# State-space stage of a decoder: the last two operations of each batch's layernorm on GpSimd instead of VectorE

## What is computed

```python
def _layernorm(x, axis=-1, eps=1e-05):
    m = jnp.mean(x, axis=axis, keepdims=True)
    v = jnp.var(x, axis=axis, keepdims=True)
    return (x - m) / jnp.sqrt(v + eps)
```

```python
BC = x @ W_in + b_in
Bm, Cm = (BC[..., :N], BC[..., N:])
dt = jax.nn.softplus((x @ W_dt1 + b_dt1) @ W_dt2 + b_dt2)
dt = jnp.clip(dt, 1e-07, 1000000.0)
tmp = A * dt[..., None]
A_bar = jnp.exp(tmp)
B_barX = jnp.expm1(tmp) / tmp * dt[..., None] * Bm[:, :, None, :] * x[..., None]
_, h = jax.lax.associative_scan(combine, (A_bar, B_barX), axis=1)
return jnp.sum(h * Cm[:, :, None, :], axis=-1) + D * x
```

## Time and profile before

| | us |
|---|---|
| three runs, median | 2016.48 |
| lowest, highest | 2016.09, 2019.49 |
| profiled execution, its own time | 2024.31 |
| its span, first to last instruction | 2022.6 |

### The profile page before, as it was taken

One profiled execution on the slowest core, in us unless ns is written; L12 is line 12 of the kernel. 1 busy time (PEld: TensorE's weight loads), 2 busy tenths in 40 slices (PEclk: granted clock), 3 DMA queues, 4 the chain that ended last, 5 costly groups with the idle time before them and its releaser, 6 DMA issues.

```text
span 2022.6 us, 34313 instructions
## 1 busy us (share of the span) xinstructions
PE 1636.8 (81%) x12460; PEld 1173.2 (58%) x12460; DVE 1373.1 (68%) x3111; ACT 1096.4 (54%) x2271; POOL 697.5 (34%) x773
## 2 busy tenths in 40 slices
PE   6588871737999788879898889988989987888864
PEld 5344431625777655567777767765559964555532
DVE  2577752137777699567999767759964456478876
ACT  4488850205777477538788345546764441147642
POOL 1344434167888302234665512220000020001238
PEclk9699975868999999986887899999999998979985
DMA  2200000110000000010000100000000000000000
GB/s 89 101 12 11 6 33 36 41 36 18 2 1 1 1 1 2 4 37 1 1 1 1 58 1 2 2 11 1 2 1 1 1 17 1 16 1 1 2 1 21
DMA packets 10422, 29.26 MB, mean 14 GB/s; under 512 B 2113, under 2 KB 6663, under 8 KB 9361
## 3 DMA queue, kind: packets, MB, share of 16 engines
q1 hardware_dynamic: 8210, 24.98, 3.5%
q0 software_dynamic: 2048, 2.12, 0.4%
HBM read 23.92 MB, written 5.24 MB: 14 GB/s over the span
## 4 chain that ended last, share of the span: by engine, by line
PE 41%; DVE 19%; POOL 13%; issue 8%; ACT 3%; DMA 0%; POOLq 0%; DVEq 0%; ACTq 0%
PE PS L1117 5%; PE PS L1199 4%; DVE negmax L2370 4%; PE PS L1259 3%; POOL big L738 3%; PE PS L1454 3%; PE PS L1465 3%; DVE V L2864 3%; POOL big L726 2%; POOL big L734 2%; PE PS L1700 2%; PE PS L1281 2%; DVE QS L2430 1%; PE PS L1174 1%; PE PS L1616 1%
## 5 line engine op out<-in xcount | busy, mean ns | idle before, releaser
L1900 ACT ACTIVATE big<-PS 128x1024 f32<-128x1024 f32 (+1 forms) x256 | 248.2, 971 | 135.8 <-PE PS L1210 135.2
L2370 DVE TENSOR_REDUCE negmax<-PS 128x4 f32<-128x1024 f32 x192 | 234.5, 1222 | 46.2 <-PE PS L1199 44.2
L630 POOL TENSOR_TENSOR rstd<-veps,mhalf 128x2 f32<-128x2 f32 x80 | 58.1, 726 | 397.9 <-DVE veps L2248 396.7
L1199 PE MATMUL PS<-KS,QS 32*128 32x256 f32 (+1 forms) x1152 | 134.8, 320 | 48.2 <-DVE negmax L2370 41.9
L1199 PEld LDWEIGHTS PS<-KS,QS 32*128 32x128 f32 x1152 | 86.5, 188 | 124.5 <-DVE negmax L2370 88.5
L1259 PE MATMUL PS<-big,V 128*32 128x256 f32 (+1 forms) x2048 | 134.4, 381 | 0.0
L1210 PE MATMUL PS<-QS,KS 32*128 32x256 f32 (+1 forms) x1152 | 133.1, 318 | 1.4 <-ACT big L1900 1.4
L1956 ACT ACTIVATE KS<-PS,NB,W 128x256 fp32r<-128x256 f32 x160 | 81.6, 561 | 78.3 <-PE PS L1117 49.2
L656 POOL TENSOR_TENSOR res<-resb,XB 128x256 f32<-128x256 f32 x24 | 17.4, 727 | 303.9 <-ACT resb L1970 303.9
L1956 ACT ACTIVATE QS<-PS,NB,W 128x256 fp32r<-128x256 f32 x160 | 81.6, 561 | 40.7 <-PE PS L1117 40.7
L1117 PE MATMUL PS<-xT,W 128*128 128x256 f32 x320 | 90.4, 407 | 13.3 <-ACT xT L1939 11.3
(11 more groups left out here) (412 smaller groups left out, 4530.5 us busy)
## 6 DMA issues: line engine op xcount, KB each, us to landing
W<-in_wpack SPq DMA_DIRECT2D x1, 4180.0 KB, 13.6
W<-in_wpack SPq DMA_DIRECT2D x1, 2836.5 KB, 9.2
W<-in_wpack SPq DMA_DIRECT2D x1, 2560.0 KB, 8.6
W<-in_wpack SPq DMA_DIRECT2D x3, 772.0 KB, 5.2
mask_i<-in_mask SPq DMA_DIRECT2D x8, 256.0 KB, 2.7
W<-in_wpack SPq DMA_DIRECT2D x1, 1798.0 KB, 6.9
x_tok<-in_x SPq DMA_DIRECT2D x1, 1024.0 KB, 4.9
ctxT<-in_ctx SPq DMA_DIRECT2D x1, 1024.0 KB, 7.7
```

Of the source, the lines that this page charges most:

```text
L1199: mm = nc.tensor.matmul(PS[:, MAXB[half], o], QS[r, bm % 2, tm, j * P:(j + 1) * P], KS[r, bm % 2, tm, k], start=not a.causal, stop=last)
L1900: nc.scalar.activation(PX[:, T % 2, 2 * p:2 * p + 2, 0:cols], PS[:, exp_banks(g)[0]:exp_banks(g)[0] + 2, 0:cols], ACT.Exp, scale=a.scale). ...
L2370: ins = nc.vector.tensor_reduce(negmax[:, h:h + 2, :].rearrange("p h j -> p (h j)"), banks.rearrange("p h (j k) -> p (h j) k", j=2), AX.X, ...
```

## The change

`norm(b)` goes from VectorE's loop, two scalar_tensor_tensor a batch at t = 4b + 7. GpSimd does the two operations at t = 4b + 6, in `root(b)`, as tensor_scalar with two per-partition scalars, behind a wait for its own root and ahead of `gains(4b+7)`. The last of them signals `x_done`.

```diff
@@ GpSimd, L2a, root(b)
                     own.step(nc.gpsimd.tensor_scalar(veps[:, :], mv[:, :, 1], 1e-5, 1.0, ALU.add, ALU.mult))
                     nc.gpsimd.tensor_tensor(rstd[:, :], veps[:, :], mhalf[:, :], ALU.pow).then_inc(sem("rstd"), 1)
+                    pool.wait_ge(sem("rstd"), before(n, "rstd") + b + 1)
+                    for j in range(2):
+                        ins = nc.gpsimd.tensor_scalar(x_tok[:, 2 * b + j, :], res[:, j, :], mv[:, j, 0:1], rstd[:, j:j + 1],
+                                                      ALU.subtract, ALU.mult)
+                    ins.then_inc(x_done, 1)
@@ VectorE, L2a
-                def norm(b):
-                    dve.wait_ge(sem("rstd"), before(n, "rstd") + b + 1)
-                    for j in range(2):
-                        ins = nc.vector.scalar_tensor_tensor(x_tok[:, 2 * b + j, :], res[:, j, :], mv[:, j, 0:1],
-                                                             rstd[:, j:j + 1].broadcast_to([P, P]), ALU.subtract, ALU.mult)
-                    ins.then_inc(x_done, 1)
-
                 for t in range(SCAN_FIRST, SCAN_LAST):
                     if t == 4 * B:
                         scalings("L2x")
-                    if (b := due(t, SCAN_DONE, 4)) is not None:
-                        norm(b)
                     if (b := due(t, SCAN_Y, 4)) is not None:
                         residual(b)
```

## The result

The changed kernel took 2036.65 us, median of four runs (2030.53 to 2037.42), against 2017.34 (2016.09 to 2019.49) for the kernel before. The ratio on record is 1.0074, 95% interval 1.0044 to 1.0104 (it isn't the quotient of the two medians, which is 1.0096): slower by both, where I had forecast 2012.3 us and a range up to 2018.0. The changed kernel run once more gave 2033.35 (2030.03 to 2037.78) against 2019.01 for 20 runs of before, ratio 1.0079 (1.0066 to 1.0092). The profiled execution took 2030.53 us, the lowest of the four, its span 2028.7; the other three took 2036.1 to 2037.4, and no profile of such a run was kept.

The account below looks back on a forecast made before the run. VectorE was taken to set the pace of the state-space loop, TensorE close behind. Terms -5.25 + 0.24 + 0 + 0 + 0.8 = -4.2 us gave 2020.1 profiled, carried over to 2012.3 us; range 2010.4 to 2018.0.

Parts of the forecast that it names:

- I carry the difference over: Whole kernel: the three-run median lies 7.8 us below the profiled execution, so 2020.1 there becomes 2012.3.
- the sum: State-space stage: -5.25 + 0.24 + 0 + 0 + 0.8 = -4.2 us, giving 2020.1 for the profiled execution.
- D: Batch loop: GpSimd keeps the port, L2771 waits for the multiply, +1.1 in each of five batches; 2023.5 us; chance 0.16.
- Parts 1 to 3: Batches 0 to 4: 1.05 us a batch saved, 0.53 from removal on VectorE, 0.52 from the port freed sooner; -5.25.
- Part 4: Batch 5, no scan_ratio behind it: +0.24 if the scan asks first, +2.2 more if the next multiply does.
- Part 5: Batch 6: last scan starts 1.38 us later, hidden behind TensorE's sums; taken as 0, upper end 1.0.
- Part 6: Batch 7: pair ends 1.1 us later than VectorE's, but next stage's start hangs on the residual; 0.
- Part 7: Batches 0 to 4: the earlier feed waits for TensorE, 0.5 us at the tightest, 0.3 for the other four; +0.8.

Follow-up runs that it names:

- scan 27 first: The changed kernel with one wait: gains(28) on GpSimd held until the scan of step 27 is done; median 2017.09 us, ratio 1.0003 to before.

## Why the prediction was wrong

**The step that failed** is the sentence under the sum, "I carry the difference over": I took everything outside the stage as a fixed length that moves along. L3a isn't fixed. It has two lengths 13 us apart, and less than a microsecond of work ahead of it moved a kernel from one to the other. The nine timed runs of the changed kernel were all at 2030 us or more; of the 24 of the unchanged kernel beside them one was (2030.8). For the profiled execution the sum gave 2020.1 us and 2030.53 was measured, 10.4 more: 13.1 from L3a and 3.7 from the stage (0.5 gained and not 4.2), less 5.0 ahead of the stage and 1.5 in the stages behind it other than L3a. From the profiled execution to the median I took off 7.8 us; the changed kernel's median lies 6.1 above its profiled execution, and these 13.9 us stay open, since its runs at 2036 and 2037 have no profile.

**A second step failed, and L3a covers it up**: parts 4 and 5 of the sum, +0.24 and 0, measured +5.24 and +1.29. They turn the -5.63 of batches 0 to 4 into +0.90. The -0.5 us of the first pair is luck, for scan 4 was hit in the kernel before. Against the two profiles of the unchanged stage without a stretched scan (245.5 and 245.6 us) the changed stage is 2 to 3 us longer.

The shift was too large for any of my rivals: D (2023.5, slower) was the nearest in sign, and its mechanism did not happen.

By its own parts:

- *Parts 1 to 3, batches 0 to 4*: -5.25 forecast, -5.63 measured, and the mechanism as described but for L2776. The pair ended 1.38 us after the scan (I had 1.45). L2776 started 0.21 us ahead of that end and still took 0.42 us, where I had it wait and end 0.28 behind the pair; L2778 waited, with 0.67 us. The reciprocal was undisturbed. Rival D, at 0.16, was wrong at its own point of decision: L2776 started at 1050.10, ahead of the multiply's 1050.32.
- *Part 4, batch 5*: I took +0.24 and named +2.2 as the other end. The other end came, in all five profiles in which GpSimd did batch 5's pair ahead of the multiply and without the added wait: scan 27 took 4.47 or 4.48 us. My reason, that GpSimd has a memset ahead, was wrong: the multiply started 0.02 us before the scan did. Steps 27 and 28 grew by 2.4 us, as this other end has it. What I had not priced is TensorE behind it: 3.51 us without work, then half rate, 2.86 us more in step 29, and 5.24 us in all over steps 27 to 29.
- *Part 5, batch 6*: step 31 grew by 1.29 (1.38 forecast). I took 0 for its effect on the stage; I have no run that isolates it.
- *Part 6, batch 7*: right but for some tenths. The pair ran from 1144.91 to 1146.48 us and L2x was 210.2 us against 209.8.
- *Part 7, TensorE's slack*, +0.8: not visible as such. In the changed kernel's first profile all five steps were at 7.88 or 7.89, so VectorE did not wait for TensorE there; no run shows the 0.8. The one collision, at step 16 (+1.55), is the same kind of event as in before at step 4.
- *The sum for the stage*: -4.2 forecast; -0.5 and -1.0 in two profiles. Without the last three batches it is -9.0 to -9.1, of which the five steps explain 5.6 and 2.6 lie behind the last scan (8.6 us against 11.2); this went with a higher clock of TensorE, 0.83 against 0.78, and wasn't tested apart. L2x gave 1.4 of it back. The same unchanged stage was 245.5 to 248.7 us in four profiles, so a forecast for it can't be better than about 3 us.

The sentence of the Trainium skill that I weighed, from "Perfetto Trace Analysis", section "Optimizing Scalar/DVE Operations", says that offloading between VectorE and GpSimd might not help because of the shared port. On the steps that the change touches the trace agrees: +0.90 us net. But it is a balance and no rule for each place: beside the 0.52 us for VectorE's two instructions, the order on the port gave 0.61 us in each of five batches, and batches 5 and 6 cost 6.5 us together. Of the 13 us in L3a it says nothing.

## What to carry to other kernels

Before a gain of a few us is carried over to the whole kernel, look for stretches further on in which TensorE is the bound and its granted clock changes within the stage: their length need not be fixed (L3a's wasn't), and a delay of one small instruction ahead of them is a cheap test of it. A move between VectorE and GpSimd should be placed step by step: the same pair of operations gains where a port-bound operation would have waited anyway and loses where it pushes a multiply up against the next scan, so move the batches that gain and leave the others. When two orders start within some hundredths of a us, take the bad one as likely: here, at scan 27, it came in five profiles of five. And compare several profiles of a stage before a difference of 1 us in it is called a gain.

## What the runs showed of the hardware that I had not expected

- L3a, with the same instructions, took 104.8 to 105.9 or 118.4 to 119.1 us, with a mean granted clock of 0.89 to 0.90 or 0.79 to 0.80. Adding about 0.8 us ahead of it took 13 us off the total. The level went with when the clock rose to full behind L3a's entry, 3.1 to 4.3 us or 4.4 to 5.2 us. What in the run-up sets that was not settled, and it varies from run to run: the unchanged kernel had 1 run of 20, 3 of 29 and 5 of 29 at 2030 us or more. The Trainium skill, "TensorE: Matmul & The Clock Gate", section "Part 1: The HAM clock gate", says that the gate's watch over the activity runs free of the kernel, so that the same kernel has more or fewer slow matmuls from run to run, and that the penalty of warming up is under 1% of a typical span. These runs fit it: the times of one kernel spread over two heights, and 13 us is 0.65% of the span. But that is three times the 4.2 us that the change was forecast to bring.
- Where a multiply on GpSimd started up to 0.05 us ahead of a scan on VectorE, the scan took nearly the whole of the multiply on top of its own time: 4.46 to 4.48 us for a scan of 2.28 beside a multiply of 2.35, at steps 16, 27 and 28 alike.
- TensorE after 3.51 us without work ran eight matmuls in 3.75 us instead of 1.99, at a granted clock of 0.50; after 1.32 us without work (the kernel with scan 27 first) in 1.96.
